# Attention and FFN on one core: the item loops of three engines written out

## What is computed

```python
q, k, v = x @ Wq.T, x @ Wk.T, x @ Wv.T          # 16 heads of 32
attn = softmax(q @ k.T / sqrt(32)) @ v
x = layernorm(x + attn)
w = (weights >= 0) * 2 - 1
x = layernorm(x + clip((x @ w.T) * scale + bias, -100, 100))
```

## Time and profile before

| | |
|---|---|
| time, median of three runs | 2921.0 us (2919.51 to 2922.0) |
| span of the profiled execution | 2917.2 us |
| difference of the two | 3.8 us |
| `project` | from 0 to about 598 us |
| `attend` | from about 598 to 2633 us; first exp at 610.4, last one ends at 2622.9 |
| `normalise_and_ffn` | from about 2634 us to the end |
| busy share of the span | PE 95%, DVE 80%, ACT 79%, POOL 12% |

### The profile page before, as it was taken

The page is one execution under the profiler, slowest core; times in us unless marked ns, Lnnn a source line. Parts: engine busy times, 40 slices in busy tenths (PEclk is TensorE's granted clock), DMA queues, the critical chain, the costliest instruction groups (busy, mean ns, idle before and its releaser), DMA issues.

```text
span 2917.2 us, 79173 instructions
## 1 busy us (share of the span) xinstructions
PE 2785.6 (95%) x29276; PEld 1423.5 (49%) x29276; DVE 2319.8 (80%) x2050; ACT 2300.0 (79%) x2789; POOL 343.1 (12%) x342
## 2 busy tenths in 40 slices
PE   8999999979999999999999999999999999997998
PEld 7888888833333333333333333344343333335887
DVE  4334343469898898989889899898989989897998
ACT  3333333379999999999999999999999999894665
POOL 0000000010000000000000000000000000004665
PEclk9999999989999999999999999999999999998999
DMA  5544445556675766767576675767667576655553
GB/s 190 182 179 173 173 173 180 182 134 144 143 160 117 166 130 140 154 138 153 119 168 128 141 164 123 160 121 162 137 142 167 117 161 134 132 122 182 187 206 130
DMA packets 223563, 445.69 MB, mean 153 GB/s; under 512 B 15442, under 2 KB 130130, under 8 KB 198868
## 3 DMA queue, kind: packets, MB, share of 16 engines
q0 software_dynamic: 27504, 200.29, 35.6%
q1 hardware_dynamic: 186596, 224.71, 24.7%
q10 hardware_dynamic: 9216, 16.78, 1.5%
HBM read 123.47 MB, written 117.96 MB: 83 GB/s over the span
## 4 chain that ended last, share of the span: by engine, by line
PE 73%; issue 4%; ACT 2%; DVE 1%; POOL 0%; ACTq 0%; DMA 0%; SPq 0%; DVEq 0%; POOLq 0%
PE banks L637 33%; PE banks L666 30%; PE banks L1008 6%; PE banks L683 2%; ACT probs L764 1%; PE banks L997 1%; PE banks L990 1%; PE banks L1004 1%; ACT L764 0%; POOL score_rows L587 0%; PE banks L991 0%; DVE partial L821 0%; ACT y L1026 0%; DVE stats L1071 0%; DVE score_rows L773 0%
## 5 line engine op out<-in xcount | busy, mean ns | idle before, releaser
L764 ACT ACTIVATE probs<-banks 128x1024 f32<-128x1024 f32 x2048 | 1891.9, 1149 | 99.6 <-PE banks L637 95.3
L637 PE MATMUL banks<-score_rows 97*32 97x512 f16 x16384 | 1186.8, 384 | 90.1 <-issue 65.8
L666 PE MATMUL banks<-probs,v_keys 128*32 128x512 f32 x8192 | 1094.5, 598 | 3.4 <-issue 3.1
L637 PEld LDWEIGHTS banks<-score_rows 97*32 97x32 f16 x16384 | 431.6, 95 | 1076.1 <-ACT probs L764 578.0
L821 DVE TENSOR_TENSOR partial<-partial,probs 128x2048 f32<-128x2048 f32 x384 | 879.7, 2291 | 50.0 <-ACT probs L764 37.7
L818 DVE TENSOR_TENSOR partial<-probs 128x2048 f32<-128x2048 f32 x192 | 440.2, 2293 | 78.6 <-ACT probs L764 74.0
L606 POOL DMA_DIRECT2D total<-partial x191 | 164.9, 863 | 1847.8 <-DVE partial L821 865.5
L666 PEld LDWEIGHTS banks<-probs,v_keys 128*32 128x32 f32 x8192 | 287.3, 112 | 181.3 <-issue 9.5
L821 DVE TENSOR_TENSOR total<-total,probs 128x2048 f32<-128x2048 f32 x128 | 292.7, 2287 | 2.6
L348 DVE TENSOR_TENSOR qk_lo<-banks,qk_hi 128x512 f16<-128x512 f32 x128 | 88.5, 692 | 240.8 <-ACT qk_hi L292 240.8
L292 ACT ACTIVATE qk_hi<-banks 128x512 f16<-128x512 f32 x128 | 76.4, 597 | 234.2 <-PE banks L246 234.2
(11 more groups left out here) (94 smaller groups left out, 2164.1 us busy)
## 6 DMA issues: line engine op xcount, KB each, us to landing
total<-partial POOLq DMA_DIRECT2D x191, 1024.0 KB, 8.2
x_in<-in_L_attn_x SPq DMA_DIRECT2D x17, 1024.0 KB, 7.3
scratch_q_raw<-qk_raw SPq DMA_DIRECT2D x16, 1024.0 KB, 5.5
scratch_k_raw<-qk_raw SPq DMA_DIRECT2D x16, 1024.0 KB, 5.6
scratch_v<-v_out SPq DMA_DIRECT2D x16, 1024.0 KB, 5.0
score_rows<-scratch_q_hi SPq DMA_DIRECT2D x128, 128.0 KB, 6.4
score_rows<-scratch_k_hi SPq DMA_DIRECT2D x128, 128.0 KB, 3.8
v_keys<-scratch_v SPq DMA_DIRECT2D x64, 256.0 KB, 6.9
```

The lines of the kernel that those rows point to most:

```text
L637: last = nc.tensor.matmul(scores_of(unit)[part, i, :], k_rows[:, h, keys], q_rows[:, h, qb * BLK:(qb + 1) * BLK], start=True, stop=True)
L666: last = nc.tensor.matmul(banks[rows, out_bank(qb), :], v_keys[:, kt, rows], probs[:, kt % P_RING, h, :], start=(kt == 0), stop=(kt == KT ...
L764: nc.scalar.activation(probs[:, kt % P_RING, heads, :], scores_of(qb * UNITS + u), ACT.Exp, scale=SCALE / GAIN ** 2).then_inc(a_prob, 1)
```

## The change

On the usual path PE's loop over items 0 to 14 becomes 15 copies of the body in straight code; the exact path keeps its loop. ACT's loop over 16 items becomes 16 copies. DVE's item 0 and its loop over 15 become 16 copies. In all of them `it` is now a number, so that every wait compares with a constant. No operation on data, no transfer and no order of work on an engine is changed. SP and POOL keep their loops.

```diff
@@ -711,8 +711,12 @@
             for kt in range(LAG):
                 scores(0, 0, kt)
             steps(scores, 0, 0, range(HEAD))
-            with nc.Fori(0, ITEMS - 1, engines=[pe.engine], hint_back_edge=True) as it:
-                item(scores, it)
+            if scores is fast_scores:
+                for it in range(ITEMS - 1):
+                    item(scores, it)
+            else:
+                with nc.Fori(0, ITEMS - 1, engines=[pe.engine], hint_back_edge=True) as it:
+                    item(scores, it)
             item(scores, LAST)
 
         needed = pe.value_load(flag[0:1, 0:1])
@@ -764,7 +768,7 @@
                     nc.scalar.activation(probs[:, kt % P_RING, heads, :], scores_of(qb * UNITS + u), ACT.Exp,
                                          scale=SCALE / GAIN ** 2).then_inc(a_prob, 1)
 
-        with nc.Fori(0, ITEMS, engines=[act.engine], hint_back_edge=True) as it:
+        for it in range(ITEMS):
             item(it)
 
     @block.vector
@@ -824,9 +828,8 @@
                     if kt == DEN_AFTER and not (first and qb == 0):
                         copy_den(st - 1, (qb - 1) % 2)
 
-        item(0, True)
-        with nc.Fori(1, ITEMS, engines=[dve.engine], hint_back_edge=True) as it:
-            item(it, False)
+        for it in range(ITEMS):
+            item(it, it == 0)
         copy_out(ITEMS * QB - 1, 1)
         copy_den(ITEMS * QB - 1, 1)
 
```

## The result

The changed kernel takes 2798.0 us (median of four, 2795.3 to 2800.6) against 2921.5 us: a ratio of 0.9583, interval 0.9569 to 0.9596. It is 123.5 us faster. The forecast was 2810 us, 111 us faster, in a range from 2801 to 2842.

A forecast was written before the change was run, and what follows sets the result against it. ACT's exp stream, interrupted by late PE instructions and table loads, bounds the kernel. 16 items x 118.8 us end the last exp 111 us earlier; 2917.2 - 111 = 2806.2, plus 3.8 between span and median, gives 2810 us, range 2801 to 2842.

The forecast's parts named there:

- The list by parts: Attention stage: table loads 21, back edges with clock echo and exit about 60, other PE stall 25, smaller breaks 5 us.
- ACT's fetching: ACT's straight code must fetch instructions anew for each item: taken as 0, bounds 0 to 122 us.
- rivals 1 to 5: PE stalls partly stay, 0.14; late ACT/DVE streams, 0.05; merges bound, 0.04; ACT fetches all miss, slower, 0.03; smaller effect, 0.03.
- The 0.26 us per query block stays, at the same size: ACT's idle where PE fits in the denominators was to remain, with query blocks 29.70 us apart.
- gains nothing of its own: On PE, removing the sequencer's arithmetic ahead of waits was put at no gain, since PE waits for ACT.
- item 15: Already straight code on PE: no "issue" idle in 87 us, blocks 29.70 us apart; taken to show what straight code does.
- The 1.3 of the first load that stays: ACT's first table load was to remain ahead of the first exp, 1.3 us subtracted from the gain.
- The start stall: Item 0 was to keep ACT's 1.09 us of idle at 617.11, 1.3 us with the lost overlap.
- the cost of the back edge: ACT's loss per item when PE's loop body starts anew: 2.70 + 1.26 + 0.3 = 4.3 us.
- the other stall: PE's "issue" idle some 26 us ahead of the branch, costing ACT 1.65 us per item, absent in item 15.
- a unit's 16 matmuls: PE's idle cuts this group in two, taken as a sign that no wait in the code is there.
- Rival 1: PE's stall away from the branch and smaller breaks come from block borders and stay: 2840 us, chance 0.14.

The follow-up runs named there:

- e1_pe: The kernel before with PE's loop alone written out, ACT and DVE keeping their loops: 2827.8 us (ratio 0.9690).
- e4_pe_act: The kernel before with PE's and ACT's loops written out, DVE keeping its loop: 2799.5 us (ratio 0.9592).
- e10_act_reg2: The whole change, but ACT's 16 straight bodies count items from a register loaded from memory: 2815.6 us (ratio 0.9640).
- e6_pe_regs: The whole change, with PE's straight code in a loop of one pass, which became constants when built: 2797.3 us (ratio 0.9570).
- e7_act_regs: The whole change, with ACT's straight code in a loop of one pass, which became constants when built: 2797.0 us (ratio 0.9571).
- e14_dummy: The whole change plus 192 unused register instructions per item on PE, which were dropped when built: 2799.5 us (ratio 0.9589).
- e9_pe_reg2: The whole change, but PE's 15 straight bodies count items from a register loaded from memory, without a branch: 2853.8 us (ratio 0.9764).
- e16_chain: The whole change plus 192 register additions per item kept in PE's stream, those waits still comparing with constants: 2858.4 us (ratio 0.9785).

## Why the prediction was right or wrong

**Right.** The bound: ACT's stream with what interrupts it, read from one item of its timeline. PE's part was forecast at 90 us and is 91.8 alone, and the new item with it alone is the forecast one. (The list by parts is loose: 14 back edges of 4.3 us fill its 60 us without the exit's 6, and no row stands behind its 5 us of smaller breaks; with the one and without the other PE's part is 91 us.) 15 table loads were forecast at 21 us: they cost 1.4 us each in `e1_pe`, and ACT's part alone is 23.2. The Trainium skill (ScalarE: Activation LUTs, section What ACT_TABLE_LOAD costs) gives 2.66 us for a switch to a different set. Here the load comes back between exps alone, and the row of 1.28 us without a drain was right, against the prediction's estimate of 40 us from that page. DVE's back edge was put at 0: right beside the other two. ACT's fetching, put at 0 by its first pass, cost nothing, with 40 packets. None of the rivals 1 to 5 happened.

**Wrong, and by how much.** The time lies 3 us below the range and 12 us below the forecast. On the profiled executions, from PE's first scores (607.90 and 605.80 us) to the last exp's end (2622.95 and 2503.27) the stage got 117.6 us shorter; the forecast was 111.0. Three terms make the 6.6 us between.

- "The 0.26 us per query block stays, at the same size", and removed sequencer arithmetic "gains nothing of its own". This step failed: the two sentences took the sequencers' arithmetic to cost nothing. It was drawn from item 15, where PE alone runs straight code and ACT still computes for its waits. ACT written out makes the item 118.53 instead of 118.8 us, 16 x 0.27 = 4.3 us. That it is ACT's arithmetic is shown from both sides: the pace stays with ACT in its loop (`e1_pe`), goes down with it written out (`e4_pe_act`), and goes above the old one with a loaded register and no loop (`e10_act_reg2`).
- "The 1.3 of the first load that stays": the load moved ahead of the first scores, where ACT waits, and 1.4 us went (first exp 1.09 us behind PE's first scores, 2.51 before).
- The start stall, taken over at 1.3 us, shrank to 0.4 us.

The other 6 us are outside the stage, where "the stages ahead and behind don't change" put nothing: PE's first scores came 2.1 us earlier, and what follows the last exp took 4.0 us less (294.3 and 290.2 us). The cause stays open. In all the traces, whose code there is the same, the first scores come from 605.7 to 610.2 us and the tail takes 290.0 to 295.9 us; in `e6_pe_regs`, `e7_act_regs` and `e14_dummy`, which are the changed kernel again, the tail took 293.8, 290.0 and 290.2 us. So single executions differ by most of it. The medians of these kernels are 2797.0 to 2799.5 us.

The stage's 6.6 us alone would have left 2803 us, inside the range; the time fell out of it with the 6 us outside. The low end, 9 us below the forecast, had room for a pace off by 0.1 us per block, but it had no case in which ACT's own waits cost something and none for the other stages.

**Right in sum, wrong in cause.** PE's idle was put down to the loop: "the cost of the back edge", 4.3 us per item, and of the other stall nothing was known but that straight code hadn't it. So the 91.8 us came out right by some luck: whichever of the two makes the stalls, writing the loop out removes both. Item 15 differs in two things, the loop and the register instructions, and the prediction looked at the first. `e9_pe_reg2` and `e16_chain` have no branch, and with register instructions the item rises from 118.5 to 122.5 and 122.2 us. That "removing arithmetic of the sequencer gains nothing of its own" was therefore wrong on PE as well, by 60 us in `e16_chain`. The prediction's sign that the idle cuts "a unit's 16 matmuls" counts wrongly, since a unit has 8, but a cut behind 6 or 7 of them is inside a unit all the same. The Trainium skill's rule on a taken branch (Runtime: NRT & Kernel Launch, section Instruction fetch mechanics) fits the stall at the branch, which the hint cuts from 4.8 to 2.5 us. Its sentence that fetching is hidden behind the rate of issue doesn't hold for the streams with register instructions (44 us of "issue" idle in `e16_chain`), and holds for the one without (none in 1860 us). Rival 1 had it that block borders alone make the stalls; they do so only with such additional instructions in the stream.

**Open.** Why a register instruction makes the next block's fetch late isn't shown by any run, nor that another kind of instruction would not. Nor is how PE's 91.8 us, 6.1 per item, divide: register instructions without a branch make some 4 us, which leaves 2 us for the branch, but the kernel with a third of the branches lost more than that would give (2897 against 2854 us). DVE's 6 us when written out alone are measured and not explained.

## What to carry to other kernels

A loop that a sequencer runs can cost more than its branch: look for idle that is put down to "issue" in the middle of a group of matmuls, spaced like the instruction packets, and count the register instructions in that stream. When straight code elsewhere in the same trace is taken as the model of the new one, list everything in which the two differ, on every engine that stands on the path. A function table that is loaded once per pass of a loop is found in one line of the profile.

## What the runs showed of the hardware that was not expected

- Register additions in PE's stream, 192 per item, with all waits on constants and no branch, brought back 44 us of "issue" idle and 60 us of time (2858.4 against 2798.0 us).
- Waits on a register on ACT add 0.08 us of idle or more at each break, although ACT is waiting for PE there (0.26 against 0.18 us or less).
- With register instructions in its stream and no branch, all 47 "issue" idles of PE in `e9_pe_reg2` stand whole multiples of 256 instructions apart, at some of the block borders and not at all of them (198 packets in the same 1860 us).
- On DVE it is the other way: an addition that waits for its predecessor starts 2.40 us after it with a constant and 2.32 us with a register.
- The hint for the back edge was worth 46 us in a loop of 15 passes (2966.7 against 2920.6 us), and nothing that can be measured in one of 5 passes (2894.9 without, 2897.0 with).
